# Routing, row scatter and biases of a mixture-of-experts layer moved into the loop ahead of it

## The chip, the cores and the metric

The kernel runs on 1 core of one Trainium2 chip. The metric is the device time in microseconds of one execution; before the change it is 1098.29 us, the median of 3 runs (1097.12 to 1099.25).

## The reference

A two-layer Perceiver on x (16 sequences x 64 rows x 256 features; 1024 rows in all) with a context of 256 rows per sequence. Layer 0: masked cross attention, self attention with a rotary part, a dense expert mixture. Layer 1: cross attention, a state-space layer, and a block of causal "latent" attention and a mixture of experts with top-2 routing. Only the last part is touched:

```
h = x + attention(rms_norm(x, norm1_w), Wq, Wk, Wv, Wo)
h = h + moe(rms_norm(h, norm2_w), ...)
# moe(x):
logits = x @ router_w + router_b
topv, topi = top_k(logits, 2);  topw = softmax(topv)
h1 = einsum('bsd,edf->ebsf', x, W1) + b1
h2 = einsum('bsd,edf->ebsf', x, W2) + b2
eo = einsum('ebsf,efd->ebsd', h2 * silu(h1), W3) + b3
out = sum over the two chosen experts of topw * eo
```

There are 8 experts of width 1024. Each row goes to two of them.

## The kernel before

The 1024 rows are 8 tiles of 128 (`TILES`). Every engine has a program of its own, and the engines meet at semaphores: `hold(eng, signal, n)` waits until the signal has been given n times, and `Chain.link` lets VectorE or GpSimd wait for its own last operation. The stages follow each other as ln, xa0 (first cross attention, 16 steps over the sequences), sa, ffn, xa1, ssm, rope, la (latent attention), moe.

**la** (`inner("la")`) is a loop of `INNER_STEPS` = 12 steps on every engine. Tile i is projected in step i, scored and exponentiated in i + 1, turned and mixed with the values in i + 2, projected out and normalised in i + 3 (`xn`, VectorE), and turned into `XT` by TensorE (`turn`) and ScalarE in i + 4, where ScalarE and GpSimd also split the normalised row into two f16 halves, `row_parts` (L1129, L1364). VectorE's step k is, in this order: `gather_outputs(k - 3)` (L1678, L1682), `scale_probs(k - 2)`, `sum_values(k - 1)`, `row_maxima(k - 1)` (L1650, L1658), the residual of tile k - 3, `copy_queries_and_keys(k)`, `normalise` of tile k - 3 (L1714). GpSimd computes the reciprocal root, adds the residual to x and splits, in every step, one or two of the 96 pieces of the expert weights into f16 halves (L1297, L1298); SP stores each piece to `w_parts` in DRAM and loads the next. When the last piece is stored, SP loads the split weights of experts 0, 1, 2 (3 MB each, L438) into a ring of three places; later experts follow as a place comes free.

**Routing** comes after la. TensorE multiplies all tiles by `router_w` (L906), VectorE finds the two best experts of each row (L1868 to L1885), TensorE ranks the rows within their experts by products with a triangular matrix and with ones (L913 to L918), and VectorE works out how many blocks of 128 rows each expert gets, which expert owns each block, and each row's two places in the blocks (L1891 to L1920). GpSimd then scatters the f16 rows to these places in `x_rows` in DRAM, 16 indirect DMAs (L1455); ScalarE waits for all of them, loads the rows of the first 8 blocks (`load_rows`, L1206) and copies the first turned block (`take_rows`, L1214). Meanwhile TensorE and VectorE add the weighted `b3` to x (L923 to L937), and VectorE splits `b1` and `b2` into f16 halves (L1943 to L1946).

**The blocks.** TensorE runs, for b = 0 to 24: `turn_block(b + 1)` (L940), `hidden(b)` (4 bias products L957 against a one-hot `choice` of the block's expert, then 24 products L967 to L969), `turn_hidden(b - 1)` (L979), `down(b - 2)` (24 products L990 to L992). `hidden(b)` writes PSUM banks that VectorE must have read: it waits for `gated_done`, the product of silu(h1) and h2 of block b - 1 (L1966, two halves). VectorE's step b is `choose_biases(b + 1)` (L1952), L1966 for block b, L1974 (the low half of the hidden rows) for block b - 1. ScalarE copies the turned rows, computes silu (L1240), the high halves (L1247) and copies the sums out (L1222). The sums go to `y_rows`, and at the end GpSimd gathers each row's two results (L1461) and VectorE adds them by their weights (L1982, L1984).

## Time and profile before

| | |
|---|---|
| median of 3 runs | 1098.29 us |
| the profiled execution's own time | 1096.61 us |
| its span in the trace | 1094.7 us |
| PE busy | 839.2 us (77%) |
| DVE busy | 548.9 us (50%) |
| ACT busy | 446.4 us (41%) |
| POOL busy | 397.8 us (36%) |
| chain of waits, largest shares | PE 45%, ACT 15%, DVE 15%, POOL 10%, issue 9%, DMA 4% |

All times of the trace are microseconds from the start of the span. PE is TensorE, DVE VectorE, ACT ScalarE, POOL GpSimd; SPq, ACTq are the queues from which SP and ScalarE issue DMAs. A busy share over the whole span mixes stages with different limits; the chain of waits, followed back from the last instruction, names what each stage waited for. la runs from about 686 to 800, the routing and the scatter from 800 to 841, the blocks from 848 to 1067.

### The profile page before, as it was taken

The numbers are of one execution on the slowest core, as the hardware profiler recorded it, in microseconds if no ns is written. First come the engines' busy times: TensorE is split into PE (matmuls) and PEld (weight loads), VectorE is DVE, ScalarE is ACT, GpSimd is POOL, SyncE is SP. The second block draws the span as 40 slices with busy tenths as digits, with TensorE's granted clock in tenths as the row PEclk, the third lists the DMA queues.
The fourth block names the chain that finished last, engine by engine and source line by source line (L and its number), as shares of the span: only waits on it lengthen the run. The fifth ranks groups of instructions, "written<-read, shape, count | busy, mean of one in ns | idle before, by whom it ended". The sixth has DMA issues, their size and how long they took to land.

```text
span 1094.7 us, 21754 instructions
## 1 busy us (share of the span) xinstructions
PE 839.2 (77%) x6944; PEld 590.6 (54%) x6944; DVE 548.9 (50%) x1397; ACT 446.4 (41%) x1527; POOL 397.8 (36%) x577
## 2 busy tenths in 40 slices
PE   1899989689879658888987462677453999999990
PEld 0666666478754226666665341566341466666660
DVE  2477777568744343655655577576432222222222
ACT  1566666346614224656564102466400233333320
POOL 3356465535458754243344534222425000000005
PEclk9999999899969888999998765777655999999995
DMA  8121112633241634343233200211167034443004
GB/s 320 42 56 46 49 48 65 237 104 109 88 154 46 196 105 136 104 137 106 96 106 123 97 0 12 86 40 40 49 229 279 16 132 153 145 140 131 16 21 120
DMA packets 63723, 114.37 MB, mean 104 GB/s; under 512 B 6304, under 2 KB 20384, under 8 KB 62880
## 3 DMA queue, kind: packets, MB, share of 16 engines
q1 hardware_dynamic: 55488, 103.15, 28.0%
q10 hardware_dynamic: 6624, 6.03, 1.7%
q0 software_dynamic: 1536, 4.20, 1.3%
q8 instruction: 45, 0.74, 0.3%
q14 instruction: 30, 0.25, 0.1%
HBM read 79.02 MB, written 34.34 MB: 104 GB/s over the span
## 4 chain that ended last, share of the span: by engine, by line
PE 45%; ACT 15%; DVE 15%; POOL 10%; issue 9%; DMA 4%; SPq 1%; DVEq 0%; ACTq 0%; POOLq 0%
ACT probs L1116 6%; PE ps L967 4%; PE ps L969 4%; PE ps L968 4%; PE ps L524 3%; ACT probs L1075 3%; PE ps L567 3%; PE ps L583 2%; DMA ctx_t<-in_ctx 2%; DVE stat L1478 2%; PE ps L990 2%; PE ps L992 2%; PE ps L991 2%; ACT probs L1066 2%; PE ps L979 2%
## 5 line engine op out<-in xcount | busy, mean ns | idle before, releaser
L1266 POOL TENSOR_TENSOR var<-mv,half 128x1 f32<-128x1 f32 x56 | 11.0, 196 | 288.5 <-DVE mv L1479 201.2
L1298 POOL TENSOR_TENSOR piece_out<-piece_in,piece_out 128x512 f16<-128x512 f32 x96 | 112.7, 1173 | 7.7
L1966 DVE TENSOR_TENSOR probs<-ps,ctx_t 128x512 f32<-128x512 f32 x46 | 29.6, 686 | 155.0 <-PE ps L969 155.0
L567 PE MATMUL ps<-pack_const,probs 128*128 128x128 f32 x512 | 78.7, 291 | 28.8 <-DVE vbuf L1520 11.3
L1461 POOL DMA_INDIRECT pt<-y_rows,neg x16 | 15.4, 962 | 234.2 <-DMA y_rows<-vbuf 229.7
L1323 POOL TENSOR_TENSOR probs<-probs,gp 128x512 f32<-128x512 f32 x64 | 81.3, 1303 | 51.1 <-ACT probs L1066 51.1
L567 PEld LDWEIGHTS ps<-pack_const,probs 128*128 128x128 f32 x512 | 58.7, 146 | 53.2 <-DVE vbuf L1520 13.1
L1297 POOL CAST piece_out<-piece_in 128x512 f16<-128x512 f32 x96 | 62.2, 648 | 41.9 <-DMA piece_in<-in_w 40.7
L967 PE MATMUL ps<-arena,qbuf 128*128 x184 | 71.0, 386 | 0.0
L968 PE MATMUL ps<-arena,qbuf 128*128 x184 | 70.8, 385 | 0.0
L969 PE MATMUL ps<-arena,qbuf 128*128 x184 | 70.8, 385 | 0.0
L524 PE MATMUL ps<-ctx_t,arena 128*128 128x256 f32 x256 | 64.1, 394 | 8.4 <-DMA ctx_t<-in_ctx 6.3
L1527 DVE COPY pt<-ps 128x512 f32<-128x512 f32 x64 | 44.3, 692 | 49.6 <-PE ps L567 49.6
L1066 ACT ACTIVATE probs<-probs,mx 128x256 f32<-128x256 f32 x128 | 63.2, 497 | 12.9 <-DVE mx L1552 12.9
L536 PE MATMUL ps<-arena,ctx_t 128*128 128x256 f32 x256 | 63.5, 390 | 0.0
L1075 ACT ACTIVATE probs<-ps,mx 128x256 f32<-128x256 f32 x128 | 58.7, 492 | 8.4 <-DVE mx L1563 8.4
L524 PEld LDWEIGHTS ps<-ctx_t,arena 128*128 128x128 f32 x256 | 47.2, 195 | 20.7 <-issue 13.1
L815 PE MATMUL ps<-xt_all,arena 128*128 128x512 f32 x128 | 58.3, 610 | 0.0
L1055 ACT ACTIVATE pt<-ps 128x512 f32<-128x512 f32 x64 | 38.9, 608 | 46.4 <-PE ps L567 46.4
L473 PE MATMUL ps<-pack_const,xn 128*128 128x128 f32 x64 | 16.8, 354 | 46.3 <-DVE xn L1483 27.5
L536 PEld LDWEIGHTS ps<-arena,ctx_t 128*128 128x128 f32 x256 | 46.3, 189 | 10.9 <-issue 5.6
L990 PE MATMUL ps<-arena,pt 128*128 x184 | 50.2, 273 | 0.7 <-ACT vbuf L1222 0.7
(246 smaller groups left out, 2000.3 us busy)
## 6 DMA issues: line engine op xcount, KB each, us to landing
piece_in<-in_w SPq DMA_DIRECT2D x96, 256.0 KB, 2.8
w_parts<-piece_out SPq DMA_DIRECT2D x96, 256.0 KB, 2.0
arena<-w_parts SPq DMA_DIRECT2D x8, 3072.0 KB, 12.6
ctx_t<-in_ctx SPq DMA_DIRECT2D x32, 256.0 KB, 2.7
x_rows<-piece_out SPq DMA_DIRECT2D x1, 2944.0 KB, 16.7
qbuf<-x_rows ACTq DMA_DIRECT2D x23, 128.0 KB, 2.5
y_rows<-vbuf ACTq DMA_DIRECT2D x23, 128.0 KB, 1.7
arena<-in_xa SPq DMA_DIRECT2D x2, 1282.0 KB, 7.1
```

The source lines that it names most:

```text
L524: last = pe.matmul(AB[:, hf * KEYS:(hf + 1) * KEYS], wk[:, k, hf * P:(hf + 1) * P], c[:, k, :], start=k == 0, stop=k == DC - 1)
L536: last = pe.matmul(AB[:, 512 + kt * D:512 + (kt + 1) * D], c[:, k, kt * P:(kt + 1) * P], wv[:, k, :], start=k == 0, stop=k == DC - 1)
L567: last = pe.transpose(AB[:, o:o + P], pr[:, 2 * c + n, kt * P:(kt + 1) * P], ident)
L967: pe.matmul(bank, hi, w_hi, start=False, stop=False, skip_group_check=True)
L968: pe.matmul(bank, lo, w_hi, start=False, stop=False, skip_group_check=True)
L969: last = pe.matmul(bank, hi, w_lo, start=False, stop=k == DC - 1, skip_group_check=True)
L990: pe.matmul(block_sums, hi, w_hi, start=f == 0, stop=False)
L1066: act.activation(p, p, ACT.Exp, bias=mx[:, s * HEADS + n:s * HEADS + n + 1], scale=-1.0, accum_out=ssum[:, s * HEADS + n:s * HEADS + n + 1])\
L1075: last = act.activation(probs[:, s * 2048 + n * KEYS:s * 2048 + (n + 1) * KEYS], S[:, o:o + KEYS], ACT.Exp, bias=mx[:, s * HEADS + n:s * H ...
L1116: last = act.activation(p, p if st == "la" else S[:, o:o + SEQ], ACT.Exp, scale=scale, bias=mx[:, s * HEADS + n:s * HEADS + n + 1], accum_ ...
L1298: pool.tensor_tensor(both[:, PIECE:], src, both[:, 0:PIECE], ALU.subtract).then_inc(piece_split, 1)
L1323: pool.tensor_tensor(p, p, gw, ALU.mult).then_inc(g["weighted"].sem, 1)
```

## The change

- *Routing in la.* The pairs of tiles (0,1), (2,3), (4,5), (6,7) are routed one by one: `route_pair` and `rank_pair` on TensorE, `choose_pair` and `spot_pair` on VectorE, `scatter_pair` on GpSimd. Pair q has its router products in step 6 + 2q and its ranks in step 7 + 2q, at the start of the step on TensorE and VectorE and at the end of GpSimd's; the steps 12 and 13 (pair 3) stand behind the loop. The rank of a row is counted with the rows of the tiles before it (`sofar`).
- *Regions.* `x_rows` has 1024 rows for each expert, so that a row's place is known without the counts of the other experts. It has 8192 rows instead of 2944; clearing it moves from one DMA behind xa0 to 16 DMAs of 512 rows within xa0's loop. The row where a block begins (`rows_of_block`) is a table that ScalarE reads by `value_load` ahead of every row load. The places in `y_rows` are worked out once the blocks are known (`place_outputs`).
- *b3.* Its products with the weights and its additions to x are gone. It lies beside b1 and b2, is split by `split_biases` in la's step 9, and `down` begins with one product of `choice` and `b3`. `choice` has three places, and its wait changes from `hidden_done` to `summed`.

```diff
@@ SP
             if "xa0" in RUN:
+                sp.wait_ge(made, 6)
                 def load_step(k, s, h):
                     if live(k, 0, SEQS):
                         load_context("xa0", k, s)
+                        sp.dma_start(x_rows[bass.ds(k * 512, 512), :].rearrange("(b p) n -> p b n", p=P),
+                                     piece_out[:, 0:2 * D].unsqueeze(1).broadcast_to([P, 4, 2 * D])).then_inc(cleared, 16)
...
+            hold(sp, G["ssm"]["resid"], TILES)
+            sp.dma_start(biases[0][:, :], t["b12"][:, 0:512]).then_inc(biases_in, 16)
+            sp.dma_start(biases[1][:, 0:D], t["b12"][:, 512:768]).then_inc(biases_in, 16)
@@ TensorE
+                def route_pair(q):
+                    hold(pe, g["xt"], 2 * q + 2)
+                    hold(pe, g["resid"], at_most(2 * q + 3, TILES))
+                    if q >= 1:
+                        pe.wait_ge(spotted, q)
+                    for i in (2 * q, 2 * q + 1):
+                        for c in range(DC):
+                            last = pe.matmul(M[:, 256 + (i % 2) * 8:264 + (i % 2) * 8], tile_of_x(i, c),
+                                             kc(W["moe"]["router_w"], 8)[:, c, :], start=c == 0, stop=c == DC - 1)
+                    last.then_inc(logits_in, 1)
+                def rank_pair(q):
+                    pe.wait_ge(chosen_in, q + 1)
+                    hold(pe, g["resid"], at_most(2 * q + 4, TILES))
+                    r = slice(16 * q, 16 * q + 16)
+                    pe.matmul(M[:, 272:288], W["const"]["before"], chosen[:, r], start=True, stop=False)
+                    last = pe.matmul(M[:, 272:288], ones[:, :], sofar[:, r], start=False, stop=True)
+                    if q == TILES // 2 - 1:
+                        last = pe.matmul(M[:, 288:296], ones[:, :], sofar[:, 64:72], start=True, stop=True)
+                    last.then_inc(ranks_in, 1)
...
+                pe.matmul(block_sums, choice[0:32, b % 3, :], bias_rows[0:32, 512:768], start=True, stop=False,
+                          skip_group_check=True)
@@ ScalarE
             def load_rows(b):
-                act.dma_start(block_rows[:, b % AHEAD, :], x_rows[b * BLOCK:(b + 1) * BLOCK, :])\
-                   .then_inc(rows_in[b % AHEAD], 16)
+                at = act.value_load(rows_of_block[0:1, b:b + 1], min_val=0, max_val=EXPERTS * TOKENS - BLOCK)
+                act.dma_start(block_rows[:, b % AHEAD, :], x_rows[bass.ds(at, BLOCK), :]).then_inc(rows_in[b % AHEAD], 16)
@@ GpSimd
+                def scatter_pair(q):
+                    pool.wait_ge(spotted, q + 1)
+                    hold(pool, g["row_lo"], 2 * q + 2)
+                    pool.wait_ge(cleared, 16 * SEQS)
+                    for i in (2 * q, 2 * q + 1):
+                        for rank in range(2):
+                            pool.indirect_dma_start(
+                                x_rows[:, :], bass.IndirectOffsetOnAxis(ap=spots[:, 2 * i + rank:2 * i + rank + 1], axis=0),
+                                row_parts[i % 2][:, i // 2 * 2 * D:(i // 2 + 1) * 2 * D], None).then_inc(scattered, 16)
@@ VectorE
+            def split_biases():
+                dve.wait_ge(biases_in, 32)
+                for at, n, whole, rest in ((0, 512, biases[0], bias_rest[0]), (512, D, biases[1], bias_rest[1])):
+                    both, lo = bias_rows[:, at:at + n], rest[:, 0:n]
+                    chain.link(dve.tensor_copy(both, whole[:, 0:n]))
+                    chain.link(dve.tensor_tensor(lo, whole[:, 0:n], both, ALU.subtract))
+                    chain.link(dve.tensor_scalar(lo, lo, K["halves"][:, 1:2], None, ALU.mult))
+                    last = dve.scalar_tensor_tensor(out=both, in0=both, scalar=K["halves"][:, 0:1], in1=lo,
+                                                    op0=ALU.mult, op1=ALU.add)
...
+                def choose_pair(q):
+                    dve.wait_ge(logits_in, q + 1)
+                    r = slice(16 * q, 16 * q + 16)
+                    chain.link(dve.tensor_tensor(by_tile(logit[:, r]), by_tile(M[:, 256:272]),
+                                                 W["moe"]["router_b"].unsqueeze(1).broadcast_to([P, 2, 8]), ALU.add))
+                    pair = [slice(8 * i, 8 * i + 8) for i in (2 * q, 2 * q + 1)]
+                    for c in pair:
+                        chain.mark(dve.max(top[:, c], logit[:, c]))
+                    chain.join()
+                    for c in pair:
+                        chain.mark(dve.max_index(topi[:, c], top[:, c], logit[:, c]))
+                    chain.join()
+                    chain.link(dve.tensor_copy(topf[:, r], topi[:, r]))
+                    for rank, dst in ((0, hot), (1, hot2)):
+                        chain.mark(dve.tensor_tensor(by_tile(dst[:, r]), K["iota"][:, 0:8].unsqueeze(1).broadcast_to([P, 2, 8]),
+                                                     by_tile(topf[:, r])[:, :, rank:rank + 1].broadcast_to([P, 2, 8]),
+                                                     ALU.is_equal))
+                    chain.join()
+                    chain.link(dve.tensor_tensor(chosen[:, r], hot[:, r], hot2[:, r], ALU.add))
+                    chain.link(dve.tensor_tensor(sofar[:, 16 * q + 8:16 * q + 16], sofar[:, 16 * q:16 * q + 8],
+                                                 chosen[:, 16 * q:16 * q + 8], ALU.add))
+                    dve.tensor_tensor(sofar[:, 16 * q + 16:16 * q + 24], sofar[:, 16 * q + 8:16 * q + 16],
+                                      chosen[:, 16 * q + 8:16 * q + 16], ALU.add).then_inc(chosen_in, 1)
+                def spot_pair(q):
+                    dve.wait_ge(ranks_in, q + 1)
+                    dve.wait_ge(chosen_in, q + 1)
+                    chain.link(dve.tensor_tensor(by_tile(places[:, r]), by_tile(M[:, 272:288]),
+                                                 K["region"].unsqueeze(1).broadcast_to([P, 2, 8]), ALU.add))
+                    spot = route[:, 592:596].rearrange("p (t r) -> p t r", r=2)
+                    for rank, src in ((0, hot), (1, hot2)):
+                        picked = route[:, 600 + 16 * rank:616 + 16 * rank]
+                        chain.link(dve.tensor_tensor(picked, places[:, r], src[:, r], ALU.mult))
+                        chain.mark(dve.tensor_reduce(spot[:, :, rank], by_tile(picked), AX.X, ALU.add))
+                    chain.join()
+                    dve.tensor_copy(spots[:, 4 * q:4 * q + 4], route[:, 592:596]).then_inc(spotted, 1)
+                    dve.wait_ge(spotted, q + 1)
+                def route_step(k):
+                    if k >= 6 and k % 2 == 0:
+                        choose_pair(k // 2 - 3)
+                    if k >= 7 and k % 2 == 1:
+                        spot_pair((k - 7) // 2)
                 for k in range(INNER_STEPS):
+                    if st == "la":
+                        route_step(k)
                     if live(k, 3, TILES):
                         gather_outputs(k - 3)
...
+                    if k == TILES + 1 and st == "la":
+                        split_biases()
...
             def choose_biases(b):
-                if b >= 2:
-                    dve.wait_ge(hidden_done, 2 * b - 2)
-                dve.tensor_scalar(choice[:, b % 2, :], owners[:, b:b + 1].broadcast_to([P, P]), K["lane"], None,
+                if b >= 3:
+                    hold(dve, G["blocks"]["summed"], b - 2)
+                dve.tensor_scalar(choice[:, b % 3, :], owners[:, b:b + 1].broadcast_to([P, P]), K["lane"], None,
                                   ALU.is_equal).then_inc(chosen_, 1)
```

## Rows read from the trace of the kernel before

**Rows 1.** Busy us by stretch: PE, PEld, DVE, ACT, POOL; clock, DMA share, GB/s.

```profile
820.00:840.00 20.00, 8.97 (x24) 4.92 (x22) 4.62 (x9) 0.00 (x0) 15.26 (x16) 0.50 0.87 329
...
900.00:1000.00 100.00, 100.00 (x686) 63.07 (x684) 27.77 (x53) 33.59 (x64) 0.00 (x0) 1.00 0.47 167
```

**Rows 2.** Chain of waits, one round of la: start, us, what.

```profile
768.62 0.61 DVE scratch L1678 x2
...
779.18 0.64 POOL probs L1364
...
780.57 0.61 DVE scratch L1678 x2
```

**Rows 3.** Chain of waits, from la's last normalisation to the last scatter.

```profile
798.03 0.71 DVE xn L1714
...
800.04 6.98 PE ps L906 x32
...
818.36 0.18 DVE neg L1920
...
819.45 1.22 POOL x_rows L1455
...
838.87 2.43 DMA x_rows<-probs,neg
```

**Rows 4.** In order of time: last piece, first weight load; then the weights' landings.

```profile
801.58 1.15 POOL L1298 TENSOR_TENSOR piece_out<-piece_in,piece_out 128x512 f16<-128x512 f32 x1
...
804.83 1.35 SPq L438 DMA_DIRECT2D arena<-w_parts  x2
...
DMA to landing us min/median/max: 11.6/12.6/19.3
```

**Rows 5.** Chain of waits, small VectorE operations of the routing.

```profile
807.38 0.66 DVE top L1871 x8
...
808.05 1.20 DVE topi L1875 x9
...
815.04 0.18 DVE kbuf L1894
```

**Rows 6.** Chain of waits, around the first blocks.

```profile
846.41 1.11 issue
...
856.00 1.30 DVE probs L1966 x2
...
857.43 0.40 PE ps L957 x4
857.83 0.32 PE ps L967
```

**Rows 7.** In order of time, VectorE: the last operation of the bias split.

```profile
843.03 0.75 DVE L1946 SCALAR_TENSOR_TENSOR qbuf<-qbuf,pack_const,probs 128x512 f16<-128x512 f16 x1
```

**Rows 8.** In order of time: from one block's down product to the next block.

```profile
948.13 0.27 PE L992 MATMUL ps<-arena,pt 128*128 x1
...
948.24 0.39 PE L940 MATMUL ps<-half_ident,qbuf 128*128 128x128 f16 x4
948.44 0.38 ACT L1222 ACTIVATE vbuf<-ps 128x256 f32<-128x256 f32 x1 [1.97 <-PE ps L992]
...
948.56 0.39 PE L957 MATMUL ps<-qbuf,vbuf 32*128 32x512 f16 x4
...
948.89 0.39 PE L967 MATMUL ps<-arena,qbuf 128*128 x1
949.11 0.38 PE L968 MATMUL ps<-arena,qbuf 128*128 x1
```

**Rows 9.** DMA issues of the page: count, KB each, us to landing.

```profile
x_rows<-piece_out SPq DMA_DIRECT2D x1, 2944.0 KB, 16.7
```

**Rows 10.** In order of time: GpSimd's first mask step, TensorE's first score products.

```profile
27.95 0.40 POOL L1315 TENSOR_SCALAR neg<-mask_i 128x256 f32<-128x256 int32 x1 [1.76 <-DMA gp<-in_gp]
...
36.71 1.15 PE L583 MATMUL ps<-kbuf,qbuf 32*128 32x256 f32 x16
```

More of the change, by code:

```diff
@@ L58 @@
     "const": {"ident": P, "par_x": 2, "par_s": 2, "par_o": 32, "iota": 24, "causal": SEQ, "tri": P, "cos": P, "sin": P,
-              "before": P, "steps": 8, "lane": 1, "halves": 2},
+              "before": P, "steps": 8, "lane": 1, "halves": 2, "region": 8, "first": 24},
     "xa0": {"wq": 512, "wk": 512, "wv": 512, "wo": 512, "bq": 2, "bk": 2, "bv": D, "bo": D},
@@ L1448, in _ @@
                 inner("la")
-            hold(pool, G["la"]["row_lo"], TILES)
-            pool.wait_ge(cleared, 16)
             pool.wait_ge(routed, 3)
-            for i in range(TILES):
-                for rank in range(2):
-                    pool.indirect_dma_start(x_rows[:, :], bass.IndirectOffsetOnAxis(ap=slots[:, 2 * i + rank:2 * i + rank + 1], axis=0),
-                                            row_parts[i % 2][:, i // 2 * 2 * D:(i // 2 + 1) * 2 * D], None).then_inc(scattered, 16)
             for s in range(2):
@@ L1599, in cross @@
                 skewed(dve, SEQS, 4, step)
+            def split_biases():
[7 more added lines that the diff above has]
+                                                    op0=ALU.mult, op1=ALU.add)
+                    if at == 0:
+                        chain.mark(last)
+                last.then_inc(biases_split, 1)
             def inner(st, scale):
@@ L1689, in inner @@
+                def route_step(k):
+                    if k >= 6 and k % 2 == 0:
+                        choose_pair(k // 2 - 3)
+                    if k >= 7 and k % 2 == 1:
+                        spot_pair((k - 7) // 2)
+                if st == "la":
+                    dve.wait_ge(*loaded["moe"])
+                    chain.link(dve.memset(sofar[:, 0:8], 0.0))
                 for k in range(INNER_STEPS):
+                    if st == "la":
+                        route_step(k)
                     if live(k, 3, TILES):
@@ L1909, in _ @@
                                      op0=ALU.mult, op1=ALU.add).then_inc(routed, 1)
-            dve.wait_ge(routed, 2)
-            place = route[:, 384:448]
-            chain.link(dve.scalar_tensor_tensor(out=by_tile(place), in0=tiles_of(starts), scalar=float(BLOCK),
-                                                in1=by_tile(S[:, 512:576]), op0=ALU.mult, op1=ALU.add))
-            spots = route[:, 576:592].rearrange("p (t r) -> p t r", r=2)
-            for rank, src in ((0, hot), (1, hot2)):
-                picked = route[:, 448 + rank * 64:512 + rank * 64]
-                chain.link(dve.tensor_tensor(picked, place, src[:, :], ALU.mult))
-                chain.mark(dve.tensor_reduce(spots[:, :, rank], by_tile(picked), AX.X, ALU.add))
@@ L1930, in _ @@
-            chain.join()
-            dve.tensor_tensor(comb[:, :], hot[:, :], hot2[:, :], ALU.add).then_inc(prep_dve, 1)
-            dve.wait_ge(prep_mm, 7)
-            dve.tensor_copy(combT[0:8, :], AB[0:8, 0:TOKENS]).then_inc(prep_dve, 1)
-            hold(dve, G["la"]["summed_up"], TILES)
-            for i in range(TILES):
-                dve.wait_ge(prep_mm, 8 + i)
-                dve.tensor_tensor(tile(x, i), sums[i % 2], tile(x, i), ALU.add).then_inc(prep_dve, 1)
-            dve.wait_ge(prep_dve, 8 + TILES)
@@ L2024, in constants @@
     c["before"] = p[:, None] < p[None, :]
+    c["region"] = np.tile(TOKENS * np.arange(EXPERTS), (P, 1))
+    c["first"] = np.tile(BLOCK * np.arange(24), (P, 1))
     c["lane"] = np.where(p % 32 < 2 * EXPERTS, p % EXPERTS, -1)[:, None]
```

159 lines of the change are left out of this document (67 added, 92 removed).

## The prediction

> **What bounds the kernel now.** I read the busy table by stretch first, to see which engine each stage runs on [rows 1]: from 900 to 1000 us the TensorE is busy 100 of 100 us at a granted clock of 1.00 (the 2.4 GHz level), so the 23 expert blocks are TensorE work with nothing to spare (686 instructions in 100 us and 64 to a block make 9.33 us a block), while from 820 to 840 it is busy 8.97 of 20 us at 0.50 (1.2 GHz), doing things that nobody waits for. That hole, from the end of the latent attention ("la") to the first block, is what the change aims at. The chain of waits then says what fills both sides. Inside la [rows 2] the chain goes round through VectorE: mask and maximum, ScalarE's exponentials, GpSimd's row work, and back to VectorE's `gather_outputs` (L1678), at once followed by probability scaling and the next mask; one round is 11.95 us. VectorE is on this loop at the start of every step. After la [rows 3]: the last normalisation (798.03), 6.98 us of router products, about 11.4 us of VectorE and TensorE routing steps until the destinations are cast (818.36), 16 scatters from 819.45, the last started at 838.87 and landed 2.43 us later, and the row loads. The first bias product of block 0 (L957) starts at 846.41 + 1.11 = 847.52 [rows 6]. I use that start as anchor: the sum is what moves it, plus what changes behind it.
>
> **Ahead of the anchor.** (a) *VectorE work put into la.* `choose_pair` runs at the start of steps 6, 8 and 10, `spot_pair` of 7 and 9, each right after `normalise` and ahead of `gather_outputs`, on the loop of [rows 2]. The TensorE parts (`route_pair`, 4 instructions of 0.22 us as in 6.98/32 [rows 3]) sit at the start of its steps, which end about 2 us before VectorE's, and cost nothing; the cover gone, they cost under 1 us a step. `choose_pair` has 11 operations in 8 dependent groups: small linked operations step on by 0.18 + 0.02 to 0.26 us, two maxima take 0.25 (eight took 0.66), two index searches 0.42 (eight took 1.20) [rows 5], in all 1.85 us. `spot_pair` has six, about 1.10. Sum 3 x 1.85 + 2 x 1.10 = 7.75 us. `split_biases` is appended to step 9, right ahead of `gather_outputs(7)`. Before, its four 512-column steps ran off the path beside the row loads, from 841.30 (838.87 + 2.43 [rows 3]) to 843.78 [rows 7], 2.48 us; the new 256-column part is taken at a little over half, 1.4. Together 3.9 us, nothing hides it. So la ends 11.65 us later; bounds 0, if VectorE had slack everywhere, and 14.
>
> The Trainium skill (Perfetto Trace Analysis, Optimizing Scalar/DVE Operations) puts the fixed cost of a VectorE operation at 60 ns on SBUF and says that the profiled latency is about twice the busy time because the second half overlaps with the next instruction; priced so, 11 operations would take some 0.9 us and la would end about 4 us earlier than I say. These operations wait for each other by semaphore, so I keep the linked steps of the rows.
>
> (b) *The routing chain.* From the last `normalise` to the first scatter it was 819.45 - 798.03 = 21.42 us. Now pair 2's destinations are known before la ends, and GpSimd scatters them right after its last piece: that piece ended at 801.58 + 1.15 = 802.73 [rows 4], and with the 0.91 us from the end of the last cast (818.54) [rows 3] to the first scatter I get 5.61 us. -15.8. Pair 3 (4 router instructions, `choose_pair`, 6 rank instructions of 0.22, `spot_pair`) is ready some 7 us after the last transposed tile, while GpSimd still sends pair 2 (5.1 us): about even, nothing to add. The block table on VectorE, 2.7 us before and some 3.9 with the new row table, ends before the last scatter lands.
>
> (c) *Scatters.* Eight instead of sixteen remain: the first and the last start lie 19.42 us apart [rows 3], 1.29 a scatter and 1.28 without the slower first; 8 x 1.28 = -10.2.
>
> (d) *Their landing.* The last landed in 2.43 us [rows 3], when the weight loads were through. Now it meets the first weight loads, which are tied to the end of la and shift with it. The nearest rows are the weights' own landings, 11.6 us on free engines and 19.3 behind each other [rows 4], for 24 times the bytes of a scatter. Its own row is the nearer one, so I take +1.5 for the crowding, bounds 0 and 4. The Trainium skill (DMA: Bandwidth & Descriptors, Queues, rings and completion order) says that a DMA engine serves its queues in turn packet by packet, so a small transfer need not wait for a whole 3 MB load; by that rule the term would be near 0 and the time 1.5 us lower. No row here shows two queues served so.
>
> (e) *Row loads by register.* Each of the eight loads ahead of `take_rows(0)` now reads its address from SBUF first. The nearest row is the 1.11 us that TensorE spent before block 0 on two such reads and their address arithmetic [rows 6]. 0.5 each makes +4.0; bounds 0.8 and 5.
>
> The weights of expert 0 don't bind: issued at 804.83, first landing 11.6 us later [rows 4]; shifted by 11.65 that is 828.1, and the row side is ready near 838. The anchor moves by 11.65 - 15.8 - 10.2 + 1.5 + 4.0 = **-8.85**, to 838.7.
>
> (f) *Elsewhere.* The clearing DMA of 2944 KB (16.7 us to landing [rows 9]) becomes 16 of 512 KB behind each context load of the first cross attention; at that rate each takes about 2.9 us of a step of about 11, and SP's first context load waits for GpSimd's memset. The only early consumer is the mask: GpSimd's first mask step already waits 1.76 us for its data at 27.95 [rows 10], and would come up to 5.8 us later, 34.1, against first scores finished at 37.86. +0.5, bounds 0 and 3. Everything that b3 did (transposes, copy, eight products, eight additions) ran beside the scatters: removing it gives 0.
>
> **Behind the anchor.** (g) *A new wait on VectorE.* `choice` is read again by the down product, so its ring has three slots and `choose_biases(b + 1)` waits until block b - 2 is **summed**. It stands at the start of VectorE's step b, and queued behind it is the product of block b's halves (L1966), which the TensorE needs before it may overwrite PSUM with block b + 1. The TensorE does `hidden(b)`, `turn_hidden(b - 1)`, `down(b - 2)`: before, L1966 ran during the last two; now it can't start until `down(b - 2)` is over. In the steady block [rows 8] the down product is over for ScalarE at 948.44, and block b + 1's bias product starts at 948.56. With the wait: 948.44, choice 0.2, L1966 1.30, hand-over 0.14, that is 950.08, 1.52 us later. [rows 6] show this very hand-over where nothing lies between, in block 0 to 1: L1966 at 856.00 for 1.30, then L957 at 857.43, and the refilled pipeline takes 0.40 where a steady one takes 0.33, and 0.32 for the next product against 0.22: +0.17. 1.69 us a block for b = 2 to 21, 20 blocks: **+33.7**; bounds 28 and 40. VectorE and ScalarE are busy 28 and 34 of 100 us there [rows 1], so their other work of a block finds room.
>
> (h) *b3 in the down product.* One product of 32 rows and 256 columns for each of 23 blocks; the last one of 256 columns before, L992, is followed after 0.11 us [rows 8]: +2.5, bounds 1 and 5.
>
> **Sum.** -8.85 + 0.5 + 33.7 + 2.5 = +27.8 us. The span of 1094.7 becomes 1122.5, the profiled execution's own time of 1096.61 becomes 1124.4; the median of the runs lies 1.7 above that, so 1126.1.
>
> **Rivals.** *R1, faster:* the wait of (g) doesn't bind. It decides at one point: whether `summed` reaches b - 1 before block b's hidden product is done. For it speaks only that I may misread the order; against it that `down(b - 2)` stands behind `hidden(b)` in TensorE's program. Then 1098.3 - 8.85 + 0.5 + 2.5 = 1092.4. *R2, the hole stays:* transfers crowd (scatters, row loads and 9 MB of weights now fall together, and la ends later), and block 0 starts at 847.5 as before: 1126.1 + 8.85 = 1135.0. *R3, the clock falls:* TensorE pauses 1.5 us in each block. In [rows 6] a pause of that length before block 1 didn't bring it down: the next products take 0.40 and 0.32 us, near the 0.33 and 0.22 of [rows 8]. The Trainium skill (TensorE: Matmul & The Clock Gate, A second HAM failure mode) tells of a kernel whose micro-pauses between groups made the clock fall and rise again. If a third of the blocks ran at 1.2 GHz, 8 x 9.3 = 74 us: 1200. *R4, la has slack:* the routing inside la costs nothing, 1126.1 - 11.65 = 1114.5; against it, [rows 2] show VectorE going from `normalise` straight on.
>
> **How the numbers follow.** The forecast has 0.74, R1 0.06, R2 0.08, R3 0.04, R4 0.08. The unknown costs taken at their ends give about 1110 and 1143; the range 1111 to 1140 holds the forecast's cases, R2 and R4 and leaves out R1, R3 and the outermost ends. A difference of 0.2% (2.2 us) is about what a measurement of this kernel can tell from none. Faster 0.06, same 0.01, slower 0.93.
>
> **What would show it.** Right: in the block stage L957 is released by L1966 in 22 blocks instead of 2, TensorE is busy about 85% at clock 1.00, and blocks are 11.1 us apart instead of 9.33; L1966 starts after the last down product; the first L957 is near 839; the last la `normalise` near 809.7; eight scatters lie behind la. Wrong: blocks still 9.33 us apart (R1), a first L957 at 847 or later (R2), a granted clock under 1 among the blocks (R3), la's end within 4 us of 798 (R4).

## The result, and the profile after

The changed kernel takes 1132.63 us (median of 4 runs, 1131.23 to 1137.74) against 1097.70 us of the kernel before beside it: 1.0323 times as long, 95% interval 1.0288 to 1.0358. The forecast was 1126.1 us, range 1111 to 1140. The profiled execution took 1131.23 us, with a span of 1129.4 us, 34.7 more than before. Of the executions of the experiments below, one of e4's ten took 1443.77 us at a mean granted clock of 0.555, where the other nine have 0.875 to 0.886; the ratios leave it out.

Lines of the changed kernel are new numbers: L2006 is the one-hot of `choose_biases`, L2022 stands where L1966 stood, L963 is the bias product (L957 before), L973 to L975 the hidden products, L985 turns the hidden rows, L992 the b3 product, L998 to L1000 the down product, L946 turns block rows, L1222 takes them.

Busy us by stretch, where [rows 1] answer (PE, PEld, DVE, ACT, POOL; clock, DMA share, GB/s):

```profile
820.00:840.00 20.00, 1.49 (x7) 1.35 (x6) 8.32 (x49) 0.21 (x1) 7.80 (x8) 0.50 0.91 323
...
900.00:1000.00 100.00, 87.00 (x585) 53.73 (x584) 24.11 (x45) 28.37 (x54) 0.00 (x0) 1.00 0.40 135
```

The hole at 820 to 840 is still there, with even less TensorE work in it, and the DMA engines are as full (0.91 against 0.87). The new loss is in the second line: TensorE had 100 of 100 us in the blocks and has 87, at the same clock. The view of what TensorE waited for, over the whole span, names who holds it:

```profile
PE ps L963 <- DVE probs L2022: 30.8, 22, 1.7
```

and one steady block in order of time shows how, first TensorE and then VectorE (to be read beside [rows 8]):

```profile
959.62 0.27 PE L1000 MATMUL ps<-arena,pt 128*128 x1
959.73 0.39 PE L946 MATMUL ps<-half_ident,qbuf 128*128 128x128 f16 x4
961.56 0.40 PE L963 MATMUL ps<-xs,vbuf 32*128 32x512 f16 x4 [1.45 <-DVE probs L2022]
```

```profile
959.93 0.29 DVE L2006 TENSOR_SCALAR vbuf<-kbuf,pack_const 128x128 f16<-128x128 f32 x1 [8.48 <-PE ps L1000]
960.13 1.28 DVE L2022 TENSOR_TENSOR probs<-ps,ctx_t 128x512 f32<-128x512 f32 x2
```

VectorE idles 8.48 us ahead of a one-hot of 0.29 us. It waits for block b - 2 to be summed, and the product that frees PSUM for the next block (L2022) stands behind it in VectorE's program. TensorE ends its last down product, turns rows, and waits 1.45 us: from the last down product to the next bias product it is 1.94 us, where [rows 8] have 0.43.

The path from the attention to the blocks, in order of time, GpSimd, then ScalarE's queue, then SP's:

```profile
819.98 1.04 POOL L1364 DMA_INDIRECT x_rows<-probs,neg  x1 [0.17 <-issue]
...
828.95 0.98 POOL L1364 DMA_INDIRECT x_rows<-probs,neg  x1 [0.30 <-issue]
```

```profile
835.20 7.79 ACTq L1215 DMA_DIRECT2D qbuf<-x_rows  x8
```

```profile
821.91 12.75 SPq L441 DMA_DIRECT2D arena<-w_parts  x3
```

GpSimd's eight last scatters run into the weight loads, which SP issues from 821.91 on. ScalarE's first address read starts at 834.3, and the row load follows 0.9 later:

```profile
L1214 ACTq TENSOR_LOAD <-neg x23: 276/281/467, 834.3 to 983.1; - x23
```

(Durations in ns: shortest, median, longest; then the first and the last start.) The last `normalise` is at 815.11 and the first bias product at 845.37. With the stage ahead of la (its first VectorE operation at 689.54 before and 691.91 after), the span is accounted for stage by stage:

| stage | before | after | difference | forecast |
|---|---|---|---|---|
| start to la's first VectorE operation | 689.54 | 691.91 | +2.37 | +0.5 (f) |
| la, to its last normalise | 108.49 | 123.20 | +14.71 | +11.65 (a) |
| to the first of the last scatters | 21.42 | 4.87 | -16.55 | -15.8 (b) |
| first to last scatter | 19.42 | 8.97 | -10.45 | -10.2 (c) |
| last scatter's start to the first row load | 2.45 | 6.25 | +3.80 | +1.5 (d) |
| row load to the first bias product | 6.20 | 10.17 | +3.97 | +4.0 (e) |
| first bias product to the end | 247.18 | 284.03 | +36.85 | +36.2 (g, h) |
| span | 1094.7 | 1129.4 | +34.7 | +27.8 |

### The profile page after: what moved, and what is told of

Read it like the earlier page. It is cut to its first block and busy times, and to the rows that moved or that the text cites. A ratio compares the mean times of both kernels' runs of the same rounds, so it can differ in the third digit from the quotient of the medians.

```text
span 1129.4 us, 21979 instructions
## 1 busy us (share of the span) xinstructions
PE 837.3 (74%) x6943; PEld 585.6 (52%) x6943; DVE 558.4 (49%) x1441; ACT 446.3 (40%) x1527; POOL 398.5 (35%) x577
## 5 line engine op out<-in xcount | busy, mean ns | idle before, releaser
L2006 DVE TENSOR_SCALAR vbuf<-kbuf,pack_const 128x128 f16<-128x128 f32 x23 | 6.6, 285 | 169.9 <-PE ps L1000 169.7
L973 PE MATMUL ps<-arena,qbuf 128*128 x184 | 70.5, 383 | 0.0
L975 PE MATMUL ps<-arena,qbuf 128*128 x184 | 70.2, 381 | 0.0
L1249 ACT ACTIVATE ctx_t<-ps 128x512 f32<-128x512 f32 x46 | 25.0, 594 | 76.8 <-PE ps L975 76.8
```

The source lines that it names most:

```text
L973: pe.matmul(bank, hi, w_hi, start=False, stop=False, skip_group_check=True)
L975: last = pe.matmul(bank, hi, w_lo, start=False, stop=k == DC - 1, skip_group_check=True)
```

## The experiments

Every trace carries some drift ahead of la: la's first VectorE operation lies between 688.2 and 696.9 us in the executions below, at different TensorE clocks. So I read each experiment by its own stages, and give the medians beside them. Each kernel's times have the kernel before beside them on the same chip (median 1097.7 to 1099.3).

**e1, a fourth choice buffer.** The changed kernel, with

```diff
-        choice = vbuf[:, 1024:1024 + 3 * BLOCK].rearrange("p (s n) -> p s n", s=3)
+        choice = vbuf[:, 1024:1024 + 4 * BLOCK].rearrange("p (s n) -> p s n", s=4)
...
-                if b >= 3:
-                    hold(dve, G["blocks"]["summed"], b - 2)
+                if b >= 4:
+                    hold(dve, G["blocks"]["summed"], b - 3)
```

> The changed kernel with four places for choice instead of three, so that choose_biases(b) waits for block b - 4 to be summed, one block earlier. Theory S (the wait for summed ahead of L2022 is the stall of the block loop): TensorE no longer pauses between blocks, blocks go from 11.16 us apart to 9.33 + 0.11 = 9.44, 20 x 1.72 = 34 us come back, about 1098 us. Rival B (the block loop is longer because of what else is new in it, the b3 product and ScalarE's row loads by register): the pause stays in part, the kernel keeps above 1115 us.

Measured 1100.32 us, 1.0024 times the kernel before (1.0006 to 1.0041), span 1098.1: 31.3 us of the 34.7 are gone. From the first Silu of block 2 to that of block 22 it is 192.7 us, 9.635 a block, against 11.16 in the changed kernel and 9.32 before. Without the pauses the change is level with the kernel before: 1.6 us slower, where the prediction had 1092.4 for a kernel whose wait doesn't bind. The move of the routing by itself gained nothing.

**e2, the wait alone in the kernel before.** Nothing of the change but its wait, with nothing to wait for:

```diff
                 if b >= 2:
                     dve.wait_ge(hidden_done, 2 * b - 2)
+                if b >= 3:
+                    hold(dve, G["blocks"]["summed"], b - 2)
```

> The kernel before with nothing but the one new wait added: choose_biases(b) also waits until block b - 3 is summed. Theory S: 20 pauses of 1.5 to 1.7 us, 30 to 34 us more, about 1130 us, with no b3 product, no register loads and no routing in the loop. Rival B: the wait alone costs under 10 us, below 1108 us.

Measured 1132.47 us, 1.0316 (1.0292 to 1.0341): the wait alone makes the kernel before as slow as the whole change. A block takes 10.917 us, so the wait costs 1.60 a block, 32.0 in 20 blocks, where I had written 1.69 and 33.7. The span grows by 33.6, of which 2.35 lie ahead of the first bias product (849.87 against 847.52), where nothing was edited, and 31.3 behind it.

**e3, e1 without the b3 product** (b3 is left out of the result):

```diff
-                pe.matmul(block_sums, choice[0:32, b % 4, :], bias_rows[0:32, 512:768], start=True, stop=False,
-                          skip_group_check=True)
```

> e1 without the one-hot product of b3 (b3 is left out of the result). Theory S: 23 x 0.11 = 2.5 us less than e1. Rival: the product with its 32-row weights costs a switch between shapes, up to 5 us less than e1; or it was covered and nothing is gained.

Measured 1094.23 us, 0.9957 (0.9935 to 0.9979), 6.1 less than e1 by the medians and 4.6 by the spans. Blocks 2 to 22 take 186.4 us, exactly as before, against 192.7 in e1: the b3 product costs 0.316 us a block, not the 0.11 of its neighbours. In order of time, TensorE in e1 and then in e3:

```profile
962.44 1.04 PE L985 MATMUL ps<-pack_const,probs 128*128 128x128 f32 x8
963.41 0.28 PE L992 MATMUL ps<-xs,vbuf 32*128 32x256 f16 x1
963.62 0.28 PE L998 MATMUL ps<-arena,pt 128*128 x1
963.74 0.27 PE L999 MATMUL ps<-arena,pt 128*128 x1
```

```profile
961.63 1.04 PE L985 MATMUL ps<-pack_const,probs 128*128 128x128 f32 x8
962.50 0.27 PE L996 MATMUL ps<-arena,pt 128*128 x1
962.61 0.27 PE L997 MATMUL ps<-arena,pt 128*128 x1
```

The product itself starts 0.97 us behind L985 instead of 0.87, and its successor comes 0.21 later instead of 0.11: 0.1 is lost on entering and 0.1 on leaving.

**e4, the bias split behind la.** e1, with `split_biases` called after `place_outputs` instead of in step 9 of la:

```diff
-                    if k == TILES + 1 and st == "la":
-                        split_biases()
...
             place_outputs()
+            split_biases()
+            chain.restart()
```

> e1 with split_biases moved from the latent attention's step 9 to VectorE's idle time behind place_outputs, where it waits for the row loads anyway. Theory L (all VectorE work put into that loop lies on the path): its 4.95 us in the trace come back in full, 5 us less than e1. Rival W: the start of block 0 is set by the landing of scatters and weights, which are tied to other things, and less than 2 us come back.

Measured 1097.46 us, 0.9987 (0.9973 to 1.0). la goes from 123.17 to 118.13 us: 5.04, all of the split's 4.95. By the spans e4 is 4.9 faster than e1, by the medians 2.9; in its trace twelve hidden products of block 0 run at 1.2 GHz instead of e1's five, which costs 1.4.

**e5, addresses read first.** e4, and ScalarE reads the eight row addresses ahead of its wait for the scatters:

```diff
             act.wait_ge(routed, 2)
+            first_rows = [act.value_load(rows_of_block[0:1, b:b + 1], min_val=0, max_val=EXPERTS * TOKENS - BLOCK)
+                          for b in range(AHEAD)]
             act.wait_ge(scattered, 16 * 2 * TILES)
```

> The kernel with four choice buffers and the bias split behind the attention (span 1093.3 us, median 1097.5), in which ScalarE reads the 8 first row addresses from SBUF ahead of its wait for the scatters, instead of one ahead of each row load. Theory: a row load preceded by its own register read takes 0.97 us of issue against 0.47 in the kernel before, and the reads (0.45 us each: 0.28 load, 0.15 address arithmetic, 0.02 assert) lie on the path between the last scatter and block 0. Ahead of the wait they are hidden: eight row loads in 3.8 us instead of 7.8, the first bias product and the end about 3.9 us earlier (span 1089.4). Rival: the eighth row load decides nothing, block 0 starts when its own rows are turned, or a load is held back by the queue and not by the reads: under 1 us.

Measured 1092.78 us, 0.9939 (0.9905 to 0.9973), span 1090.4 (1093.3 in e4). The eight loads take 3.89 us instead of 7.79, as expected, but from the last scatter's start to the first bias product it is only 14.71 us instead of 16.25: 1.5 gained, not 3.9. The loads are issued early and land late. Another 1.37 of the span is TensorE's clock: its hidden products of block 0 run at 0.63 us (1.2 GHz) for twelve products in e4 and for five in e5, before they go over to 0.38.

**e6, one weight load in flight.** e5, and

```diff
             load_expert(0)
+            sp.wait_ge(scattered, 16 * 2 * TILES)
+            sp.sem_inc(sp_passed, 1)
             load_expert(1)
```

> The same as the one before it (addresses read first), and in addition SyncE issues the second expert's weight load (3 MB) only when all scatters have landed. Theory: the last scatter takes 6.1 us from its start to the first row load because its packets share the 16 DMA engines with two weight loads of 3 MB; the same step took 2.45 us in the kernel before. With only the first expert's load in flight the step falls to 3 to 5 us: 1 to 3 us gained (span 1086.4 to 1088.4). Rival 1: the first weight load alone fills the DMA engines just as well, nothing is gained. Rival 2: the second expert's weights now come too late for its first block, PE waits and the end is later by up to 5 us.

Measured 1097.09 us, 0.9971 (0.9946 to 0.9997). The last scatter to the first row load takes 5.84 us (5.63 in e5): nothing, rival 1. Its 4.3 us over e5 by the medians lie ahead of la in the trace (694.97 against 690.06), where the edit changes nothing; why is open.

**e7, the routing in VectorE's idle time.** e6, and the three routing products go to unused columns of S, so that `route_step` can stand behind the residual sum; TensorE's part moves behind the value products of its step, and its waits with it (cut below):

```diff
-                            last = pe.matmul(M[:, 256 + (i % 2) * 8:264 + (i % 2) * 8], tile_of_x(i, c),
+                            last = pe.matmul(S[:, 768 + (i % 2) * 8:776 + (i % 2) * 8], tile_of_x(i, c),
...
-                    pe.matmul(M[:, 272:288], W["const"]["before"], chosen[:, r], start=True, stop=False)
+                    pe.matmul(S[:, 1280:1296], W["const"]["before"], chosen[:, r], start=True, stop=False)
...
                                .then_inc(g["resid"].sem, 1)
+                    if st == "la":
+                        route_step(k)
```

> The same as the one before it, and in addition the three routing products write to free PSUM columns of the score region, and VectorE takes the choosing and the spotting of a pair behind the residual sum of its step, where it sits idle for 1.7 us on the next projections and then 0.8 to 4.5 us on GpSimd, instead of at the head of the step, where nothing is idle. Theory: choose_pair (1.94 us, three times in the loop) and spot_pair (1.85, twice) lie wholly on the attention's path now and nearly wholly in the idle time then: 8 to 9.6 us gained (span about 9 us shorter than the one before it), and the product in spot_pair that took 0.92 beside GpSimd's subtraction takes 0.17 again. Rival: the gap is only nominal, since the following copy of queries and keys or the normalisation is pushed by as much: under 4 us gained.

Measured 1085.49 us, 0.9871 (0.9832 to 0.991). la falls from 118.17 to 109.84 us, 8.33, to within 1.35 us of the kernel before: the routing is nearly free in its new place.

**e8, the b3 product over all 128 rows.** e7, with b3 in the first 32 rows of its table and zeros in the others:

```diff
-                pe.matmul(block_sums, choice[0:32, b % 4, :], bias_rows[0:32, 512:768], start=True, stop=False,
+                pe.matmul(block_sums, choice[:, b % 4, :], bias_rows[:, 512:768], start=True, stop=False,
```

> The same as the one before it, and in addition the b3 product runs over all 128 rows of the one-hot (b3 stands in the first 32 rows, zeros in the others) instead of over 32 rows. In the block loop the b3 product costs 0.32 us per block (20 blocks in 192.7 us with it, 186.4 without), though its neighbours of the same 256 columns go at 0.11 us. Theory: 0.2 of it is the change of the array from 128 rows to 32 rows and back; with 128 rows it costs 0.11, and the end is 4.2 us earlier. Rival: what costs is the reading of another buffer and the opening of the sum, whatever the rows: no difference (under 0.5 us).

Measured 1081.80 us, 0.9855 (0.9811 to 0.9899). Blocks 2 to 22 take 188.57 us instead of 192.71: 4.14 less, 0.109 left per block. Four times the rows, and cheaper.

**e9, weights ahead of la.** e8, with the loads of experts 0 and 1 moved ahead of the loop of la's pieces (slots 0 and 1 of the ring are free by then), and expert 2's held back until the eighth row load has landed:

```diff
-            for c in range(LA_PIECES, EXPERTS * PIECES):
-                pass_piece(c)
...
-                sp.wait_ge(piece_stored[s], 16 * EXPERTS * PIECES // 2)
+                sp.wait_ge(piece_stored[s], 16 * PIECES)
             load_expert(0)
-            sp.wait_ge(scattered, 16 * 2 * TILES)
-            sp.sem_inc(sp_passed, 1)
             load_expert(1)
+            for c in range(LA_PIECES, EXPERTS * PIECES):
+                pass_piece(c)
...
+            sp.wait_ge(rows_in[AHEAD - 1], 16)
             load_expert(2)
```

> The same as the one before it (b3 over all rows, routing in the gap, addresses read first), but the weights of experts 0 and 1 (3 MB each) are loaded ahead of the attention, right after the state space stage, and those of expert 2 only when the eighth block of rows has landed. So nothing else is in flight while the last rows are scattered and the first rows are loaded. The last run left open why the last scatter still takes 5.8 us from its start to the first row load (2.45 in the kernel before) and the first rows 5.6 us from their load to PE (2.7 in the kernel before): with one weight load in flight instead of two nothing had changed. Theory: a single 3 MB load fills the DMA engines as well as two, and the scatter's descriptors wait in its wake: now 2.5 and 2.8 us, in all about 6 us gained (span 1071 to 1072). Rival 1: scatters that stand 0.3 us apart behind GpSimd land late by themselves, whatever else is in flight: gain under 1 us. Rival 2: the early loads hold up the pieces that GpSimd splits in the attention, whose loop gets longer by several us.

Measured 1078.15 us, 0.9812 (0.9784 to 0.9839). la stays at 109.83. The last scatter's start to the first bias product falls by 4.07 us, from 14.79 to 10.72, where a fall of 6 had been expected; the rows land in 2.05 us instead of 5.57, but the first row load comes 4.48 behind the scatter and not 2.5. The trace names the reason: the register reads, started by `routed` and not by the scatter, end at 816.1. The line of one source line's instructions (durations in ns: shortest, median, longest; first and last start), then ScalarE's queue in order of time:

```profile
L1243 ACTq TENSOR_LOAD <-neg x8: 273/277/478, 811.5 to 815.6; - x8
```

```profile
816.30 3.89 ACTq L1247 DMA_DIRECT2D qbuf<-x_rows  x8
```

**e10, two addresses.** e9, with two reads ahead of the wait, and the other six behind the taking of block 0:

```diff
-                          for b in range(AHEAD)]
+                          for b in range(2)]
...
             take_rows(0)
+            for b in range(2, AHEAD):
+                load_rows(b)
```

> The same as the one before it (weights of experts 0 and 1 loaded ahead of the attention), but ScalarE reads two addresses ahead of its wait for the scatters instead of eight, loads the rows of blocks 0 and 1, takes block 0, and reads the other six addresses behind that. In the last run the reads ran from 811.5 to 816.1 us and the first row load was issued at 816.30, 4.48 us behind the start of the last scatter (811.82), although the DMA engines were idle from about 813.8. Theory: the eight reads are now the last to end, and the scatter's own landing takes the 2.4 us of the kernel before: the first row load comes at 814.3, and the first bias product, which also waits for ScalarE to be through with all eight loads (it takes block 0 at 820.24 though PE turned it at 818.35), comes at about 819.3 instead of 822.5: 3.2 us gained (span about 1069). Rival: the scatter does take 4.4 us to land; then only the 1.9 us behind the eight loads are gained, and the row load stays at 4.4 us behind the scatter.

Measured 1080.94 us, 0.982 (0.9787 to 0.9854): no faster. The row load is at 2.59 us behind the scatter, close to the 2.45 before the change (GpSimd, ScalarE's queue and VectorE, in order of time):

```profile
820.49 0.98 POOL L1376 DMA_INDIRECT x_rows<-probs,neg  x1 [0.30 <-issue]
```

```profile
823.08 0.92 ACTq L1247 DMA_DIRECT2D qbuf<-x_rows  x2
...
828.05 6.83 ACTq L1222 DMA_DIRECT2D qbuf<-x_rows  x7
```

```profile
826.01 0.48 DVE L1638 SCALAR_TENSOR_TENSOR xs<-xs,pack_const,rot 128x256 f16<-128x256 f16 x1
```

But now the bias split, which e4 had moved here, ends last (TensorE starts at 826.76), and the seven loads in a row hold the taking of block 1 and the first Silu: the third block's bias product comes 18.57 us behind the first instead of 16.80. Only 1.0 us of this is the hold itself, a pause of 2.26 us ahead of block 1 instead of 1.25. Behind that pause the granted clock went from 1.00 (837.00 to 839.40) to 0.55 (839.40 to 843.20), and eight hidden products of block 1 run at 0.63 us (1.2 GHz), which costs 1.7; block 0 had given back 0.9, by five such products fewer than in e9. TensorE, in order of time:

```profile
839.40 0.40 PE L970 MATMUL ps<-xs,vbuf 32*128 32x512 f16 x4 [2.26 <-DVE probs L2034]
839.73 0.58 PE L980 MATMUL ps<-arena,qbuf 128*128 x1
840.11 0.63 PE L981 MATMUL ps<-arena,qbuf 128*128 x1
```

What was gained was given back two places on.

**e11, both of these undone.** e10, with `split_biases` ahead of `place_outputs`, and rows 3 to 7 loaded two at a time behind the Silus of the first blocks:

```diff
+            load_rows(2)
...
                         act.activation(gated[:, r], S[:, r], ACT.Silu).then_inc(silued, 1)
+                for late in range(3 + 2 * b, min(5 + 2 * b, AHEAD)):
+                    load_rows(late)
```

> The same as the one before it (two addresses read ahead of the scatters), with two more edits: the bias split stands ahead of the destinations of the outputs instead of behind them, and rows 3 to 7 are loaded two at a time behind the Silu of blocks 0 to 2 instead of all before the second block's rows are taken. In the last run the first row load came 2.59 us behind the last scatter's start, as forecast, but PE turned the first rows only when the bias split had ended (3.68 us behind the row load; 2.05 in the run before it), and ScalarE's six late loads (828.05 to 834.88) held the taking of block 1 and the first Silu: the second block's bias product came 9.73 us behind the first and the third 8.84 behind the second (7.16 in the run before it). Theory: both go, the first bias product comes 7.6 us behind the last scatter's start (9.18 in the last run) and the third 16.8 us behind the first (18.57): 3.3 us gained against the last run at equal times ahead of the scatters. Rival: loads spread through the first blocks come too late for block 2 or 3, and PE waits for rows there: nothing gained.

Measured 1073.51 us, 0.9785 (0.9756 to 0.9813): 59 us faster than the change and 24 faster than the kernel before. In order of time, the row load and the first bias product:

```profile
818.20 0.92 ACTq L1247 DMA_DIRECT2D qbuf<-x_rows  x2
```

```profile
823.28 0.62 PE L970 MATMUL ps<-xs,vbuf 32*128 32x512 f16 x4 [1.01 <-issue]
```

The last scatter started at 815.61, so the row load is 2.59 us behind it and the first bias product 7.67 (7.6 expected). The third block's bias product is at 839.24, 15.96 behind the first (16.8 expected); the 0.84 under the expectation is TensorE's clock, which rises some four products earlier in block 0 than in e9. The pause ahead of block 1 is 1.25 us again, and block 1 has no product at 1.2 GHz. Rows loaded late hold nobody.

## Why the prediction was right, and where its terms were off

The sign, the cause and the range were right. The median lies 6.5 us above the forecast. Of the 6.9 us that the forecast of the span lacks, 6.2 lie ahead of the first bias product. The range's lower end has no sum behind it: the low ends of (d) to (h) give 1113.7, with (a) at its 0 as well 1102, and not about 1110.

(g) **The wait on VectorE**, right, shown from both sides: taking it out of the change gives back 31.3 us (e1), putting it into the kernel before costs 33.6 us of its span (e2), 31.3 of them behind the first bias product. The mechanism is the one told: VectorE's queue, not data. The pause is sized right, 1.51 us in the changed kernel (1.94 less 0.43) and 1.58 in e2 against 1.52 forecast. The refill of 0.17 on top was a misreading: 0.40 and 0.32 in [rows 6] are lengths of pieces of the chain, 0.33 and 0.22 in [rows 8] distances from start to start. From start to start the kernel before has 0.33 and 0.23 behind its own pause (L957 at 857.43, L967 at 857.76, L968 at 857.99), so nothing is refilled. Why e2 pauses 0.07 us longer than the changed kernel is open.

(h) **The b3 product**, mis-sized: 0.316 us a block, 6.3 in 20 blocks and 7.3 in 23, not 2.5 (bound 5). I priced it like its 128-row neighbours [rows 8]; going over to 32 rows and back comes on top, and e8, where the product takes 0.109, shows that this is the whole surplus. Beside the wait it costs the same: 11.16 less 9.33 is 1.83 a block, the pause of 1.51 and 0.32. So (g) and (h), 36.2 by the forecast and 36.85 measured, came out right by luck: in 20 blocks the wait is 3.5 us under its 33.7 and b3 3.8 over its 2.5. Two more differences of 1.3 us cancel in this stage: block 0 had five hidden products at 1.2 GHz instead of twelve, and what follows block 22's Silu took longer.

(a) **Routing in la**, mis-sized: 14.71 instead of 11.65. The steps cost 1.94, 1.94 and 2.07 for `choose_pair` (1.85 forecast), 1.85 and 1.85 for `spot_pair` (1.10), 4.95 for the split (3.9). The linked steps of the rows thus held for `choose_pair`; the 0.9 us that the prediction names as another price would have been half. The nearest rows [rows 5] came from a stretch in which GpSimd did nothing. Beside GpSimd's split of a weight piece one operation of each group is stretched. VectorE first, then GpSimd, in order of time in the changed kernel, here for the third `spot_pair`, just behind la; the first two show the same 0.92 us, at 761.18 and 788.91:

```profile
815.11 0.70 DVE L1797 SCALAR_TENSOR_TENSOR xn<-xn_all,rstd,arena 128x256 f32<-128x256 f32 x1 [2.92 <-POOL probs L1383]
815.74 0.16 DVE L1750 TENSOR_TENSOR kbuf<-ps,pack_const 128x16 f32<-128x16 f32 x1
815.93 0.93 DVE L1755 TENSOR_TENSOR kbuf<-kbuf,hot 128x16 f32<-128x16 f32 x1
...
816.98 0.16 DVE L1755 TENSOR_TENSOR kbuf<-kbuf,hot 128x16 f32<-128x16 f32 x1
```

```profile
815.61 1.21 POOL L1307 TENSOR_TENSOR piece_out<-piece_in,piece_out 128x512 f16<-128x512 f32 x1
```

The same operation on 16 columns takes 0.93 and 0.16 us; the long one ends at 816.86, GpSimd's at 816.82. The first cast of the split shows the same (800.95 for 1.37 us, 0.43 in e4, where it stands behind la; GpSimd's subtraction ends at 802.03). That is 0.76 in each of the two `spot_pair` and 0.94 in the split, 2.5 of the 3.1 missing. In e8, whose `spot_pair` stands behind the residual sum, that product (L1760) takes 0.17 in the first two; the third, behind la, still takes 0.93. The rival R4, that la has slack, was wrong for this place and right for another one in the same step: e7 has the routing for 1.35 us, because VectorE idles there for TensorE and then for GpSimd. I had read that VectorE stands on the loop at the head of a step [rows 2], and not where in the step it does not.

(b), (c) **Chain and scatters**, right to 0.75 and 0.25 us.

(d) **The landing**, mis-sized: +3.8 for the stage, near the end of its bounds (0 to 4) and not at +1.5. The last 0.9 of it is the first address read, which belongs to (e); the landing itself is +2.9 (5.35 us to the start of that read, against 2.45). Cause shown: with the weights out of the way the row load follows the scatter by 2.59 us (e10, e11), close to the 2.43 before the change [rows 3]; with one load in flight or with more it is 5.3 to 6.3. The rows' own landing has the same cause (5.57 in e8, 2.05 in e9), a cost that I had nowhere. What I drew from the Trainium skill's rule (DMA: Bandwidth & Descriptors, Queues, rings and completion order), that this term would be near 0, is not borne out: whatever the order in which the engines serve their queues, here the last scatter lands 2.7 to 3.3 us later beside one 3 MB load (e6 to e8) than beside none.

(e) **Register reads**, 4.0 forecast, 3.97 measured for the stage and 4.9 with the first read. The agreement is weaker than it looks: e5 took the reads out and only 1.5 came back, since the crowded rows landed late either way. In an empty machine the reads are the bound (e9).

(f) **Elsewhere**, +0.5 forecast and +2.37 seen ahead of la, unresolved: the same place differs by 8.7 us between e9 and e10, which don't differ there, and e2, which has the kernel before unchanged up to there, starts la 2.4 us late as well (691.97). No run separates the clearing from this drift.

R1 (no binding) and R3 (the clock falls) did not come. R2 (the hole stays) came in part: the hole shrank by 2.15 us only (8.85 forecast), through (a), (d) and (f). The first bias product, at 845.37, lies nearer to R2's 847.5 than to 838.7, and the median nearer to R2's 1135.0 than to 1126.1; R2's reasons, crowded transfers and a later end of la, are what (d) and (a) show. Two of the signs that were to show the forecast right are missed, the first bias product near 839 and the last `normalise` near 809.7 (815.11). Against R3 stand the 22 pauses of up to 1.7 us ahead of L963, with a granted clock of 1.00 from 900 to 1000 us, where nine of them lie. The Trainium skill (TensorE: Matmul & The Clock Gate, A second HAM failure mode) tells of pauses between groups that made the clock fall and rise; this kernel's pauses don't. The longer one of e10, 2.26 us ahead of block 1, was followed by products at 1.2 GHz; whether its length or its place did it, no run separates.

## What to carry to other kernels

When a buffer gets a second, later reader, look at what is queued behind the wait that guards it: a ring one slot longer was worth 31 us here, more than everything the change was about. Work put into a loop costs nothing or all of itself depending on where in the step it stands; look for the engine's idle time inside one step, not for its busy share. And after each wait that is removed, ask what ends second: between the last scatter and the first block it was the landing, then the register reads, then the bias split, then a queue of loads, one behind the other. Last, take the new wait out by itself before a change is judged: here it hid that the rest of the change was worth nothing as it stood (e1), and that with its parts, the b3 product and the weight loads in better places it is 24 us faster than the kernel before (e11).

## What the runs showed of the hardware that I had not expected

**VectorE held beside GpSimd.** A 16-column product of two SBUF operands lasts 0.93 us instead of 0.17 and ends within 0.04 us of GpSimd's subtraction. A cast of 4 columns from SBUF does the same (L1758, 0.67 us from 817.38, beside GpSimd's L1383 from 817.36, 0.67 us), and one of 512 columns (L1623) ends 0.29 us behind GpSimd's operation. The sum before it (L1750), whose first operand is in PSUM, began 0.13 us behind GpSimd's operation and took its 0.16 us. The Trainium skill (SBUF — State Buffer, Who interferes with whom) says that a VectorE instruction with two SBUF inputs waits for a GpSimd instruction that reads SBUF, for all its length, that casts in a two-port mode do so too, and that others don't; this trace agrees in each of these places.

**A 32-row product between 128-row products.** 0.316 us instead of 0.109, the difference on both sides of it (e1, e3, e8). The Trainium skill (TensorEngine Tiling (Array Packing), Key Properties) says that changing the tiling mode drains TensorE; if that is what happens here, each change costs 0.1 us. The runs show the time and that it goes with the 32 rows, not the drain.

**Reading a register from SBUF.** 0.45 us on ScalarE's queue (0.28 the load, 0.15 the address, 0.02 the bound check), so that in a row of eight a load with its read follows the last by 1.05 us instead of 0.48; eight together ahead of their use took 4.6 us in e9.

**The clock's rise is not fixed to the work.** Block 0 had five hidden products at 1.2 GHz in the changed kernel and in e5 and twelve in e4, which moves the end by 1.4 us without any edit to them.

**Nor is it kept through every pause.** Ahead of block 1 TensorE paused 1.25 us in every other run here, and its next products took 0.39 us or less; in e10 it paused 2.26 us, and the next eight took 0.58 to 0.63. It is one execution.
